# Grouping TensorE's work of each attention pair by tile shape, with side products in the maxima's banks

## The reference

```
layer 0: x = x + out0 + gelu(LN(out0) @ W1 + b1) @ W2 + b2,  out0 = attention(x, ctx; 16 heads of 8) @ Wo + bo
layer 1: x = x + attention(LN(x), LN(x); 16 heads of 64) @ Wo1 + bo1
         x = x + attention(LN(x), ctx;   16 heads of 64) @ Wo2 + bo2
         x = x + (a * gelu(gate)) @ Wf + bf,  a, gate = split(LN(x) @ Wp + bp)
attention: softmax(q k^T * scale) v
```

## Time and profile before

| | |
|---|---|
| median of 3 runs | 503.56 us (503.46 to 507.79) |
| the profiled execution | 499.26 us, its span 497.5 us |
| mean granted TensorE clock | 0.983 of full |
| busy, share of the span | TensorE 95%, VectorE 49%, ScalarE 50%, GpSimd 40% |

### The profile page before, as it was taken

The page is one execution under the profiler, slowest core; times in us unless marked ns, Lnnn a source line. Parts: engine busy times, 40 slices in busy tenths (PEclk is TensorE's granted clock), DMA queues, the critical chain, the costliest instruction groups (busy, mean ns, idle before and its releaser), DMA issues.

```text
span 497.5 us, 7041 instructions
## 1 busy us (share of the span) xinstructions
PE 474.8 (95%) x2800; PEld 259.7 (52%) x2800; DVE 244.0 (49%) x469; ACT 247.5 (50%) x347; POOL 201.3 (40%) x177
## 2 busy tenths in 40 slices
PE   7989798999999999999999999999998999989896
PEld 4544354355537445444445745444574554844495
DVE  2664645556535544454766344337533356341653
ACT  3753474454563565545445255545525564246622
POOL 4440101045934873464555445753217233145010
PEclk9996998999999999999999999999998999999999
DMA  8600000000000000100000002000010000000000
GB/s 268 222 0 1 1 1 1 0 1 1 1 0 2 0 1 0 33 0 2 0 1 1 0 1 74 1 1 1 0 45 0 1 1 1 1 1 1 1 20 23
DMA packets 7857, 8.89 MB, mean 18 GB/s; under 512 B 561, under 2 KB 6129, under 8 KB 7825
## 3 DMA queue, kind: packets, MB, share of 16 engines
q1 hardware_dynamic: 7824, 8.44, 5.2%
HBM read 7.92 MB, written 0.52 MB: 17 GB/s over the span
## 4 chain that ended last, share of the span: by engine, by line
PE 88%; DVE 5%; ACT 3%; POOL 2%; issue 1%; DMA 1%; SPq 0%; DVEq 0%; POOLq 0%
PE PV L656 17%; PE ST L637 13%; PE ST L603 7%; PE M L616 6%; PE ST L704 4%; PE ST L642 4%; PE ST L591 4%; PE ST L604 4%; PE ST L625 3%; PE DEN L671 3%; PE DEN L440 2%; PE M L741 1%; PE ST L760 1%; ACT PT L1175 1%; PE ST L693 1%
## 5 line engine op out<-in xcount | busy, mean ns | idle before, releaser
L1012 POOL TENSOR_TENSOR psums<-PT 128x1024 f32<-128x1024 f32 (+1 forms) x32 | 75.7, 2367 | 140.7 <-ACT PT L1175 140.7
L1492 DVE TENSOR_REDUCE maxw<-M 128x1 f32<-128x512 f32 x128 | 82.5, 686 | 73.7 <-PE M L616 73.6
L1175 ACT ACTIVATE PT<-ST 128x1024 f32<-128x1024 f32 (+1 forms) x96 | 93.8, 1022 | 40.8 <-PE ST L642 40.8
L656 PE MATMUL PV<-PT,V 128*64 128x512 f32 (+1 forms) x384 | 93.0, 605 | 0.0
L637 PE MATMUL ST<-R 64*128 64x512 f32 (+1 forms) x576 | 84.6, 396 | 1.6 <-DVE AT L1517 0.7
L1020 POOL TENSOR_TENSOR psums<-psums,PT 128x1024 f32<-128x1024 f32 x32 | 75.9, 2373 | 22.9 <-ACT PT L1175 21.6
L637 PEld LDWEIGHTS ST<-R 64*128 64x128 f32 (+1 forms) x576 | 50.7, 172 | 14.9 <-issue 4.3
L1494 DVE TENSOR_REDUCE maxw<-M 128x2 f32<-128x308 f32 x64 | 27.7, 475 | 42.7 <-PE M L616 42.7
L656 PEld LDWEIGHTS PV<-PT,V 128*64 128x64 f32 (+1 forms) x384 | 23.3, 136 | 47.6 <-issue 42.2
L1183 ACT ACTIVATE AT<-PV 128x512 f32<-128x512 f32 x32 | 19.1, 598 | 49.3 <-PE PV L656 49.3
L616 PE MATMUL M<-R 64*128 64x512 f32 (+1 forms) x256 | 43.2, 367 | 0.1
(11 more groups left out here) (203 smaller groups left out, 620.1 us busy)
## 6 DMA issues: line engine op xcount, KB each, us to landing
Wq<-in_wq SPq DMA_DIRECT2D x2, 512.0 KB, 5.6
Wo<-in_wo SPq DMA_DIRECT2D x2, 512.0 KB, 6.0
xnT<-in_xT SPq DMA_DIRECT2D x2, 256.0 KB, 3.5
psums<-in_sel SPq DMA_DIRECT2D x1, 512.0 KB, 4.9
X<-in_x SPq DMA_DIRECT2D x1, 512.0 KB, 5.9
w<-in_w SPq DMA_DIRECT2D x2, 256.0 KB, 6.1
Wv<-in_wv SPq DMA_DIRECT2D x1, 512.0 KB, 6.9
Wk<-in_wk SPq DMA_DIRECT2D x1, 512.0 KB, 7.1
```

The lines of the kernel that those rows point to most:

```text
L656: ins = pe.matmul(PV[head(h), :], V[0:ph.KC, b * ph.NC + c, (2 * j + h) * HD:(2 * j + h + 1) * HD], PT1[0:ph.KC, g % 2, c, h, :], start=(c ...
L1012: ins = pool.tensor_tensor(s, p[:, 0], p[:, 1], ALU.add)
L1175: act.activation(PT1[0:ph.KC, g % 2, c], bank(("st", g, c))[0:ph.KC, :, :], ACT.Exp, scale=HD ** -0.5).then_inc(ph.exp, 1)
L1492: ins = dve.tensor_reduce(maxw[:, g % 2, c, HD * h:HD * h + 1], m[:, :], AX, ALU.max, negate=True)
```

## The change

Within a pair TensorE's products are put into runs of like shape: all scores of the pair with the next pair's maxima products among them; then everything on the whole array, that is side products, the projection, and further side products; then denominators and all values of this same pair (not the second half of the last one's), and the turn at the end. Side products that need one bank, and some that need two, are put in the M banks (`claim_half`, `among_maxima=True`) and share their order with the maxima. A maxima product can start inside a scores unit: `scores(g, c, unit, at)` issues it ahead of the unit's `at`-th pair of matmuls. `to_queries0` moves to the start. ScalarE, VectorE and GpSimd get orders to match: ScalarE copies the last pair's weighted values at the start of a pair, and reads most side products behind `maxima_rows(g + 1)`; VectorE does all maxima of a pair first. The feature turns of sequence 1 and of stages 2 and 3 stand at other pairs than before. The functions of the side products only get their bank from `claim_half` instead of `claim`, and their readers from `half_bank`; that part is left out here.

```diff
-        def maxima_units(g, c):
-
-            if g + 1 >= NG:
-                return []
-            if pair(g + 1)[0] is pair(g)[0]:
-                return [c]
-            return [c // 2] if c % 2 == 0 else []
+        def maxima_units(g):
+
+            return range(TB if g < NPAIR else 2)
+
+        VALUES = {6: (0, TB), 7: (0, TB + 2), 9: (1, 0), 10: (1, 1), 12: (1, 2), 13: (1, 3)}
+        SPREADS = {9: (None, 0), 10: (None, 1), 11: (2, 3), 18: (0, 1), 19: (2, None), 20: (3, None),
+                   26: (0, 1), 27: (2, 3)}
...
+            def claim_half(key, freed, count, among_maxima):
+
+                if not among_maxima:
+                    return claim(key, freed, count)[:, 0, :]
+                side[key] = len(m_uses) % 2
+                return claim_m(freed, count)[:, :]
...
-            def scores(g, c):
+            def scores(g, c, unit=None, at=0):
+
 
                 ph, i = pair(g)
+                if unit is not None and at == 0:
+                    scores_max(g + 1, unit)
                 if c == 0:
...
+            def start_attention():
 
                 project(0)
...
                 loaded("wv1")
                 for c in range(TB):
                     scores_max(0, c)
-                    values(0, c, P, xnT, Wv)
+                    values(0, c)
+                    if c in (1, 2):
+                        to_queries0(1, c - 1)
                 pe.wait_ge(consts_set, 1)
                 turn_pair(0)
-                for g in range(NG):
-                    ph, i = pair(g)
-                    for c in range(0, ph.units, 2):
-                        for k in maxima_units(g, c):
-                            scores_max(g + 1, k)
-                        scores(g, c)
-                        scores(g, c + 1)
-                        for k in maxima_units(g, c + 1):
-                            scores_max(g + 1, k)
-                        if c == 0 and g == 0:
-                            to_queries0(1, 0)
-                            to_queries0(1, 1)
-                        if c == 0 and g in (5, 6):
-                            values(0, TB + 2 * (g - 5), P, xnT, Wv)
-                        if c == 0 and g in (9, 13):
-                            loaded("wv2")
-                            values(1, 0 if g == 9 else 2, SC, ctxT, Wv[0:C, :])
-                        if c == 0 and g in (10, 11):
-                            spread_inverse(0, 2 * (g - 10))
-                        if c + 2 == ph.units:
-                            if g == 0:
-                                back0(1)
-                            if g + 2 < NG:
-                                project(g + 2)
-                            if g == 2:
-                                hidden(1)
-                            if g == 3:
-                                second(1)
-                            if g in (5, 6):
-                                values(0, TB + 2 * (g - 5) + 1, P, xnT, Wv)
-                            if g in (9, 13):
-                                values(1, 1 if g == 9 else 3, SC, ctxT, Wv[0:C, :])
-                            if g in (10, 11):
-                                spread_inverse(0, 2 * (g - 10) + 1)
-                            if g in (18, 19, 26, 27):
-                                spread_inverse(g // 8 - 1, 2 * (g % 2))
-                            if g in (12, 20):
-                                attention_out(1, g // 8 - 1)
-                            if g == 28:
-                                attention_out(2, 0)
-                        if c >= 2:
-                            weigh(g, c - 2)
-                            weigh(g, c - 1)
-                        elif g >= 1:
-                            last = pair(g - 1)[0].units
-                            weigh(g - 1, last - 2)
-                            weigh(g - 1, last - 1)
-                    if g in (18, 19, 26, 27):
-                        spread_inverse(g // 8 - 1, 2 * (g % 2) + 1)
+
+            def all_scores(g):
+
+                ph, i = pair(g)
+                if ph is self_att:
+                    narrow = g + 1 == NPAIR
+                    scores(g, 0, 0, 0)
+                    scores(g, 1, *(() if narrow else (1, 2)))
+                    scores(g, 2, 1 if narrow else 2, 3)
+                    scores(g, 3)
+                    if not narrow:
+                        scores_max(g + 1, 3)
+                else:
+                    last = g + 1 == NG
+                    scores(g, 0, *(() if last else (0, 0)))
+                    scores(g, 1)
+                    if not last:
+                        scores_max(g + 1, 1)
+
+            def side_before(g):
+
+                if g == 3:
+                    hidden(1)
+                if g in VALUES:
+                    n, t = VALUES[g]
+                    if n == 1:
+                        loaded("wv2")
+                    values(n, t)
+                if g in SPREADS and SPREADS[g][0] is not None:
+                    spread_inverse(g // 8 - 1, SPREADS[g][0])
+
+            def side_behind(g):
+
+                if g == 0:
+                    back0(1)
+                if g == 1:
+                    out0(1)
+                if g == 2:
+                    turn(0, 1)
+                if g == 4:
+                    second(1)
+                if g == 5:
+                    turn(1, 1)
+                if g in (6, 7):
+                    values(0, VALUES[g][1] + 1, True)
+                if g in SPREADS and SPREADS[g][1] is not None:
+                    spread_inverse(g // 8 - 1, SPREADS[g][1], True)
+                if g in (12, 20):
+                    attention_out(1, g // 8 - 1)
+                if g == 13:
+                    turn(2, 0)
+                if g == 28:
+                    attention_out(2, 0)
+                if g == 30:
+                    turn(3, 0)
+
+            def attention():
+
+                start_attention()
+                for g in range(NG - 1):
+                    all_scores(g)
+                    side_before(g)
+                    if g + 2 < NG:
+                        project(g + 2)
+                    side_behind(g)
                     if g >= 1:
                         denominators(g - 1)
-                    if g == 0:
-                        out0(1)
-                    if g == 1:
-                        turn(0, 1)
-                    if g == 4:
-                        turn(1, 1)
-                    if g in (13, 21):
-                        turn(2, g // 8 - 1)
-                    if g == 29:
-                        turn(3, 0)
-                    if g + 1 < NG:
-                        turn_pair(g + 1)
+                    for c in range(pair(g)[0].units):
+                        weigh(g, c)
+                    turn_pair(g + 1)
+                    if g == 21:
+                        turn(2, 1, False)
+                all_scores(NG - 1)
...
             for g in range(NG):
                 ph, i = pair(g)
-                if g == 1:
+                if g == 2:
                     normal(0, 1, O)
                     add_first(1)
-                if g == 21:
-                    normal(2, 1, X)
+                if g == 5:
+                    normal(1, 1, X)
+                    add_bias(1, "bo1", 1)
+                if g in (13, 21):
+                    normal(2, g // 8 - 1, X)
                 if g == 29:
                     normal(3, 0, X)
                 p = PT1[0:ph.KC, g % 2]
@@ -1010,17 +1053,11 @@
                 elif g == 3:
                     pool.wait_ge(o_done[0], B)
                 ins = pool.tensor_tensor(s, p[:, 0], p[:, 1], ALU.add)
-                if g in (4, 13):
+                for c in range(2, ph.NC):
                     link(ins)
-                    normal(1 if g == 4 else 2, 1 if g == 4 else 0, X)
-                for c in range(2, ph.NC):
-                    if g not in (4, 13) or c > 2:
-                        link(ins)
                     pool.wait_ge(ph.exp, ph.units * i + c + 1)
                     ins = pool.tensor_tensor(s, s, p[:, c], ALU.add)
                 ins.then_inc(ph.sum, 1)
-                if g == 4:
-                    add_bias(1, "bo1", 1)
                 if g == 14:
...
+                    if g == 22:
+                        scale_features(2, 1)
+                    if g >= 1:
+                        weighted(g - 1)
+                    if g == 2:
+                        root(0, 1)
                     for c in range(ph.units):
                         exponentials(g, c)
-                        if c == 3 and g == 0:
-                            values_bias0(1)
-                        if c == 1 and g == 1:
-                            root(0, 1)
-                        if c == 0 and g == 4:
-                            root(1, 1)
-                        if c == 1 and g in (5, 6):
-                            values(0, TB + 2 * (g - 5), P)
-                        if c == 0 and g in (13, 21):
 ```

(107 more changed lines are left out.)

97 lines of the change are left out of this document (61 added, 36 removed).

## The result

| | before | after |
|---|---|---|
| median | 504.27 us (503.46 to 507.79, 4 runs) | 514.48 us (510.44 to 517.8, 4 runs) |
| ratio | | 1.020, 95% interval 1.014 to 1.026 |
| the profiled execution | 499.26, span 497.5 us, clock 0.983 | 515.13, span 513.1 us, clock 0.967 |

The changed kernel is 2% slower (1.4 to 2.6%), and 511.3 was predicted. At one clock, 0.983, the spans are 508.1 and 497.5, 10.6 apart.

The account below looks back on a forecast made before the run. TensorE, busy 95% of the span, was taken as the bound. The terms summed to +7.8 us: 507.1 from the profiled 499.26, 511.3 on the shown median 503.56; range 506 to 516, with rivals 502 to 518.

Parts of the forecast that it names:

- A: Self-attention pairs: one values block leaves the scores' run, fewer tile-shape changes, 0.37 us saved in 15 pairs, -5.5 us.
- B: Side products moved into the full-shape run with the projection: about eight lose two shape changes, -1.6 us, bounds 0 and -3.
- D: Self pairs' four consecutive score units: TensorE stalls for banks ScalarE and VectorE must free, 0.55 us in 15 pairs, +8.2 us.
- C: Waits that go away: MLP bank, spread-inverse banks, normalised features (two of 1.42 us), two in pair 0; -4.8 us.
- D's page: Scores' run, rival that only PSUM reading rate costs: 0.08 us for each of 60 units, 4.8, total 507.9; chance 0.15.
- E: ScalarE's late side-product reads hold maxima banks at the next pair's start: +4.1 us at four places, +3.5 at two.
- F: Late first inverse of the denominators: VectorE's maxima, and so TensorE, wait once in pair 9, +3.9 us, bounds 3 and 5.
- the clock: Rival: new TensorE idle stops bring three more lower-clock stretches at 1.7 us, total 516.4 us; chance 0.17.

Follow-up runs that it names:

- kernel with all fixes: Changed kernel with ScalarE's side-product reads and inverse guess before the maxima copy, VectorE's inverse at ends of pairs 8, 16, 24, `turn(3, 0)` in a double bank: 500.74 us.
- the second attempt: Changed kernel with the second half of the last pair's values back between score units 1 and 2, maxima product 1 before and 2 behind it: 513.2 us.

## Why the prediction was right, and where its terms were off

The direction and the mechanisms were right. The size (7.8 forecast, 10.6 at equal clock, or 11.8 without the odd end of the profiled run) was nearer than its terms, and that was luck: errors on both sides cancelled.

- **A**, -5.5: 0.37 a pair. Measured 6.91 before less the 1.72 of the block moved, less 4.77 with both loads halved: 0.42 a pair, -6.3.
- **B**, -1.6, bounds 0 and -3: too small, by what is left over. The kernel with all fixes has pairs 0 to 15 shorter than before by 0.95. Taking from that A (-6.3), D (+0.8 in 15 pairs, 12.0), the waits of C and the late starts gone (-2.0), the block of values that pair 0 gained (+1.7) and the `to_queries0` that it lost (-1.2) leaves about -5 for B. That is a remainder and no run isolates it.
- **C**, -4.8: the waits of the earlier trace rows are gone. Pairs 21 and 29 are 1.98 shorter each (8.26 and 8.25 to 6.28). With the root moved alone they are 1.49 shorter; the other 0.49 is the turn of features itself, which now stands in pairs 22 and 30. Pair 22 is 0.8 shorter in spite of it (1.1 with the root alone), the clock of the earlier trace rows.
- **D**, +8.2: the term that failed in size. Measured 0.78 to 0.80 a pair, about +12. The working put the last maxima product's second half at 4.98 and the end 0.56 late. The trace has the product's first half there (185.12 - 180.14 = 4.98), but its second half waits once more, to 185.26, and the projection begins 0.42 behind that, at 5.54. I had followed the chain up to the last product and let the run end with it. The late start of each product was seen, but not that VectorE, idle for 0.32 to 0.35 in each round, never takes up the lag: 1.64 a round.
- **D's page.** The rate of reading alone, 1.22 against 1.14 for a unit, gave 0.32 a pair; the row gives 0.78. The Trainium skill, TensorEngine Tiling (Array Packing), Performance Considerations, is right that the bound moves to the reading of PSUM; taken as a rate it gives less than half of the loss. By the rows of pair 5 the hand-over between the engines (0.32 to 0.35 a round) is in the loop as well, and so are the exponentials (0.21 with half of them left out).
- **E**, +4.1 and +3.5: mechanism and places as said, waits of 0.84, 0.93 (three) and 1.76 (two). The two-bank waits were nearly exact (1.82 a pair, 1.76 worked out). The one-bank ones cost 1.4 each: the first half of pair 3's maxima product began at 147.41 and the scores at 148.94 instead of 147.41 + 0.33, the 1.2 of the working, and these six matmuls took 1.10 instead of 0.86, which I had left out.
- **F**, +3.9, bounds 3 and 5: 3.33 of stop, and then 1.7 at the low clock, the rival *the clock*, which came at this place in this profile, and in the second attempt also behind a wait of 1.76. It isn't the whole loss: at one mean clock the spans are 10.6 or more apart.
- **Missed.** ScalarE's guess of the inverse stands in front of the weighted values and the exponentials of pairs 17 and 25. I had called these covered, and looked only at VectorE. The timeline of the kernel after in pair 17:

```profile
355.12 0.63 ACT L1233 ACTIVATE work<-work 128x512 f32<-128x512 f32 x1
355.66 0.58 ACT L1225 ACTIVATE AT<-PV 128x512 f32<-128x512 f32 x1
...
356.14 1.92 ACT L1217 ACTIVATE PT<-ST 77x1024 f32<-77x1024 f32 x2
...
357.20 1.13 PE L619 MATMUL ST<-xnT,Wq 128*128 128x512 f32 x2 [0.81 <-ACT PT L1217]
...
467.55 0.63 PE L489 MATMUL M<-ident,XC 128*128 128x128 f32 x4 [0.65 <-DVE maxw L1535]
```

  Twice 0.8. The last row is the other miss: `turn(3, 0)` in a maxima bank waits for the reductions in pair 30, which is 1.0 longer: 0.56 of it goes with another bank (the run with all fixes), the rest is the turn that now stands there. The start's +2.2 for the moved `to_queries0` was the third; I had only counted the wait that it left behind in pair 0.

What was too small on the side of loss (D by 4, the start by 2.2, guess and turn by 2.6, E and F by 1 each) and on the side of gain (B by 3 and more, C and A by 2, 1.2 for the `to_queries0` that left pair 0) cancelled in the greater part. About 4 of loss was left over them, and 1.2 of that the odd end of the profiled run hid.

## What to carry to other kernels

A block of work that costs a change of tile shape may be the cover of a loop between two engines: price what it hides (here 0.8) before what it costs (0.4), also at the place that it leaves (put back, it gave 0.8 us in all and not 5.5, since VectorE's last work lost its cover), and follow the loop to the consumer of its last product, not to its last product. A bank borrowed from another queue is given back when its reader runs, so the reader must stand in front of whatever waits for the next pair: six reads moved in front of one copy gave 9 us in their pairs. A wait at a pair's beginning belongs to the end of the pair before; change that one. And take out the cheap wait first: one root taken a pair earlier in the kernel before gave as much as the whole rearrangement.
